# A two-layer MoE block on one Trainium2 core: how GpSimd gathers and scatters the expert rows

## The reference

```python
x = x + _L0_conv_ref(_ln_c(x), ...)            # attention and projection
t = _to_tokens(x)                              # 1536 rows of 256
t = t + _L0_ffn_ref(_ln_t(t), gate_w, gate_b, w1, b1, w2, b2)
...
# _L0_ffn_ref: top 2 of 8 experts, F = 1024
for i in range(e):
    h = jax.nn.silu(xf @ w1[i] + b1[i])
    out = out + (h @ w2[i] + b2[i]) * comb[:, i:i + 1]
# _L1_ffn_ref: top 2 of 8 experts, I = 672, gated
for e in range(E):
    a, g = jnp.split(x @ W1[e] + b1[e], 2, axis=-1)
    out = out + cw[:, e:e + 1] * (a * silu(g) @ W2[e] + b2[e])
```

## Time and profile before

| | |
|---|---|
| median of three runs | 581.94 us (581.19 to 582.55) |
| the profiled execution, its own time | 580.54 us |
| its span, first to last instruction | 578.8 us |
| PE busy | 535.1 us (92% of the span) |
| POOL busy | 275.2 us (48%) |
| DVE, ACT busy | 340.5 us (59%), 346.4 us (60%) |
| TensorE's mean granted clock, share of full | 0.974 |
| DMA, HBM read and written | 57.55 MB and 13.47 MB |

### The profile page before, as it was taken

The page is one execution under the profiler, slowest core; times in us unless marked ns, Lnnn a source line. Parts: engine busy times, 40 slices in busy tenths (PEclk is TensorE's granted clock), DMA queues, the critical chain, the costliest instruction groups (busy, mean ns, idle before and its releaser), DMA issues.

```text
span 578.8 us, 15638 instructions
## 1 busy us (share of the span) xinstructions
PE 535.1 (92%) x3521; PEld 471.4 (81%) x3522; DVE 340.5 (59%) x791; ACT 346.4 (60%) x676; POOL 275.2 (48%) x331
## 2 busy tenths in 40 slices
PE   8999968999999999999979996899999998999991
PEld 4887527999999889998868882599999998999881
DVE  5448864456533555554785488555777574667440
ACT  4777525666655666665468655456766765566430
POOL 4639131455655366664616340335465555444432
PEclk9999979999999999999989999799999999999996
DMA  8435867346432554236432157712547383222110
GB/s 274 147 118 160 265 190 247 105 118 155 113 74 35 142 118 89 34 82 175 141 121 95 57 153 264 258 33 43 136 129 190 80 226 86 36 75 46 27 24 10
DMA packets 49034, 70.50 MB, mean 122 GB/s; under 512 B 9182, under 2 KB 40560, under 8 KB 49008
## 3 DMA queue, kind: packets, MB, share of 16 engines
q1 hardware_dynamic: 35216, 56.41, 30.9%
q0 software_dynamic: 10464, 13.58, 13.8%
q10 hardware_dynamic: 3328, 0.20, 0.4%
HBM read 57.55 MB, written 13.47 MB: 123 GB/s over the span
## 4 chain that ended last, share of the span: by engine, by line
PE 63%; DMA 11%; DVE 9%; issue 6%; ACT 4%; POOL 2%; DVEq 1%; POOLq 1%; ACTq 0%; SPq 0%
PE banks L1302 14%; PE banks L1304 14%; PE banks L1303 14%; PE banks L1515 5%; PE banks L1343 5%; DMA out_dram<-expert_io,scol 5%; PE banks L1417 2%; DVE stats L909 2%; DMA expert_io<-xn_dram,gcol 2%; PE banks L1480 2%; DMA mid_dram<-expert_io,scol 1%; PE banks L1354 1%; ACT onehot_blk L805 1%; DVE xres L1060 1%; DMA xres<-in_x_dram 1%
## 5 line engine op out<-in xcount | busy, mean ns | idle before, releaser
L1302 PE MATMUL banks<-w_hi,xT_hi 128*128 x336 | 119.5, 356 | 4.1 <-DVE xT_lo L1175 2.6
L1304 PE MATMUL banks<-w_hi,xT_lo 128*128 x336 | 115.0, 342 | 0.0
L1303 PE MATMUL banks<-w_lo,xT_hi 128*128 x336 | 114.3, 340 | 0.0
L1302 PE MATMUL banks<-w_hi,hT_hi 128*128 x364 | 108.6, 298 | 3.1 <-DVE hT_lo L1250 3.0
L1304 PE MATMUL banks<-w_hi,hT_lo 128*128 x364 | 103.2, 284 | 0.0
L1303 PE MATMUL banks<-w_lo,hT_hi 128*128 x364 | 103.1, 283 | 0.0
L611 POOL TENSOR_TENSOR w_lo<-raw,w_hi 128x1024 fp32r<-128x1024 f32 (+2 forms) x24 | 58.9, 2468 | 50.8 <-ACT w_hi L688 43.2
L829 ACT COPY banks<-seed_rows 128x672 f32 (+1 forms) x84 | 69.0, 822 | 20.2 <-DVE h_sb L1267 9.1
L1302 PEld LDWEIGHTS banks<-w_hi,hT_hi 128*128 128x128 f32 x364 | 69.5, 191 | 6.8 <-issue 5.6
L627 POOL DMA_INDIRECT expert_io<-xn_dram,gcol x52 | 53.7, 1033 | 41.7 <-POOL gcol L623 37.7
L850 ACT CAST hT_hi<-banks 128x512 fp32r<-128x512 f32 (+1 forms) x112 | 55.4, 535 | 26.1 <-PE banks L1515 23.5
(11 more groups left out here) (208 smaller groups left out, 918.7 us busy)
## 6 DMA issues: line engine op xcount, KB each, us to landing
raw<-in_L_ffn_w_dram SPq DMA_DIRECT2D x32, 512.0 KB, 3.8
raw<-in_L_ffn_W_dram SPq DMA_DIRECT2D x16, 672.0 KB, 4.0
seed_rows<-in_L_ffn_b_dram SPq DMA_DIRECT2D x8, 672.0 KB
seed_rows<-in_L_ffn_b_dram SPq DMA_DIRECT2D x8, 512.0 KB
xn_dram<-raw SPq DMA_DIRECT2D x6, 512.0 KB, 3.0
raw<-in_L_ffn_W_dram SPq DMA_DIRECT2D x8, 384.0 KB, 3.4
raw<-in_L_ffn_W_dram SPq DMA_DIRECT2D x8, 256.0 KB
wqkv<-in_L_conv_W_qkv_dram SPq DMA_DIRECT2D x2, 768.0 KB, 6.6
```

Source lines behind the costliest of these rows:

```text
L1302: pe.matmul(out, hi, w_high, start=first, stop=False, skip_group_check=onto)
L1303: pe.matmul(out, hi, w_low, start=False, stop=False, skip_group_check=onto)
L1304: return pe.matmul(out, lo, w_high, start=False, stop=last, skip_group_check=onto)
```

## The change

- GpSimd no longer copies a row buffer: the scatter reads `y_rows` itself (`y_half`). `y_out` and `y_moved` are gone. VectorE now waits, before it writes a row buffer again, until the scatter that read it has landed (`added`).
- In `scatter`, the copy of the row numbers and the wait for VectorE's rows come before the wait for the scatter before; `scol` has four columns.
- Gathered rows have two buffers, the halves of `xg`, which blocks use in turn. `gather(b)` waits for the transposition of block `b - 2` instead of `b - 1`.
- Since which half is used is written into the instructions, the loops of GpSimd and TensorE do two blocks a turn. TensorE's conditional loop has two `If`s a turn and begins at step 22; GpSimd's conditional steps are written out, one after another.
- The last two blocks go to `last_y` in both layers; in layer 1 GpSimd scatters them from there.
- Four bias rows are in SBUF instead of three (`SEED_ROWS`). After that of expert 0, SP waits for both first gathers and then loads and awaits the other three, one after another; the weights of expert 4 come behind them. Later the bias row of expert `e - 1` goes with the weights of expert `e`, and only the last one is loaded by itself. `kT` moves into `region_d`.

```diff
@@ sync: after the rows are stored
                 load_seed(L, 0)
                 seed_loaded()
-                for e in range(1, SLOTS):
+                sp.wait_ge(s.gathered_first, 16)
+                sp.wait_ge(s.gathered, 16)
+                for e in range(1, SEED_ROWS):
                     load_seed(L, e)
-                for e in range(1, SLOTS):
                     seed_loaded()
                 expert_loaded(L, 0)
-                sp.wait_ge(s.gathered, 16)
                 load_expert(L, SLOTS + 1, 1)
...
-                            load_seed(L, e - 2)
+                            load_seed(L, e - 1)
...
-                for e in range(E - 2, E):
-                    sp.wait_ge(s.w_lo, PIECES * e + 1)
-                    load_seed(L, e)
-                    seed_loaded()
+                sp.wait_ge(s.w_lo, PIECES * (E - 2) + 1)
+                load_seed(L, E - 1)
+                seed_loaded()
@@ gpsimd
-                def gather(b):
+                def gather(b, half):
                     if after(b, 2):
-                        pool.wait_ge(s.xT_mm, b)
+                        pool.wait_ge(s.xT_mm, b - 1)
...
-                def scatter(b):
+                def scatter(b, rows, n):
+                    pool.tensor_copy(scol[:, n:n + 1], col(scatter_tab, b)).then_inc(s.scol, 1)
+                    pool.wait_ge(s.scol, b + 1)
+                    pool.wait_ge(s.e_sb, b + 1)
                     if after(b, 1):
                         pool.wait_ge(s.added, 16 * b)
-                    else:
-                        pool.wait_ge(s.tab, 3)
-                    pool.tensor_copy(scol[:, :], col(scatter_tab, b)).then_inc(s.scol, 1)
-                    pool.wait_ge(s.scol, b + 1)
-                    pool.wait_ge(s.e_sb, b + 1)
-                    pool.tensor_copy(y_out, y_sb(b)).then_inc(s.y_moved, 1)
-                    pool.wait_ge(s.y_moved, b + 1)
                     pool.sem_inc(rows_go, 1)
...
+                with pool.Fori(2, MIN_BLOCKS - 2, 2) as b:
+                    step(b)
+                    step(b + 1, 1)
+                for n in range(MIN_BLOCKS - 2, MAX_BLOCKS - 1):
+                    with pool.If(blocks > n + 1):
...
+                if L == 1:
+                    for n in range(2):
+                        scatter(blocks - 2 + n, last_y[n], 2 + n)
@@ vector
-                        if after(b, 3):
-                            dve.wait_ge(s.y_moved, b - 2)
-                        rows = xg if last else y_sb(b - 1)
-                        if L == 0 and (last or left == 1):
+                        if last or left == 1:
                             rows = last_y[int(last)]
+                        else:
+                            rows = y_sb(b - 1)
+                            if after(b, 3):
+                                dve.wait_ge(s.added, 16 * (b - 2))
@@ tensor
-                steps(pe, 2, 1, blocks, step)
+                with pe.Fori(2, MIN_BLOCKS - 2, 2) as b:
+                    step(b, 1)
+                    step(b + 1, 0)
+                with pe.Fori(MIN_BLOCKS - 2, MAX_BLOCKS, 2) as b:
+                    for n in range(2):
+                        with pe.If(b + n + 1 < blocks):
+                            step(b + n, 1 - n)
+                        with pe.Else():
+                            pe.nop()
```

83 lines of the change are left out of this document (39 added, 44 removed).

## The result

The changed kernel takes **572.06 us** (median of 4 runs, 571.91 to 572.61) against 582.25 us for the kernel before (4 runs beside it, 581.19 to 584.26): ratio 0.9847, 95% interval 0.9809 to 0.9885. The forecast was 575.2 us with a range of 572.0 to 580.3. The gain is 9.9 us counted from 581.94, the median that the forecast started from, and 6.7 had been forecast. The interval of the ratio is 6.7 to 11.1 us of gain, so the prediction's 0.2% for what a measurement can tell was too small.

The account below looks back on a forecast made before the run. TensorE, busy 92% of the span, was taken to set the time, with gains only where it waits for gathers and at the end. 5.0 + 0.8 + 0.6 - 0.2 + 0.5 = 6.7 us off 581.94 gave 575.2, range 572.0 to 580.3.

Parts of the forecast that it names:

- Layer 1 between blocks 2 and 27: Waits for gathers and the half clock behind block 18's stall go: 5.0 us gained, between 0 and about 6.
- Gather 18: Layer 1: issued some 2 us earlier, near 482.3, and landed by 485.2, before the bias row's load of 485.43 starts.
- Rival 1: Layer 1, block 18: the gather still meets the bias row's load, stall and clock remain; 2.4 us won, 579.5; chance 0.17.
- Layer 0 between blocks 3 and 27: Most of the 1.1 us lost in waits for gathers goes: 0.8 us gained; moved loads over first scatters cost 0.2.
- Start of layer 0: Waits of blocks 0 and 2 for their gathers, 0.37 and 0.29 us, both go: 0.6 us gained.
- Between the layers: Start of layer 1: no such idle time before its block 0 as in layer 0, so 0 gained.
- VectorE's new wait: Before writing block b, scatter b - 2 must have landed; 3.3 us to spare at the nearest row, so 0.
- rival 4: VectorE waits for scatters at each of about six bulk loads, 1 us each: 581.2, no change; chance 0.08.
- TensorE's loops: Fewer loop branches against more false `If`s after the last block: bounded by +0.6 to -0.6 us, taken as 0.
- Rival 3: TensorE's longer loop body waits for instruction fetch each turn of layer 1: 7.5 us, gain gone, 582.7; chance 0.04.
- The end: Row copy and hand-over leave the chain behind the last rows; last scatters start 0.5 us earlier, between 0.4 and 0.8.
- Rival 2: Start of each layer: moved loads hold scatter 0, making gather 4 late; 8.2 us lost, 583.4; chance 0.09.

Follow-up runs that it names:

- late gathers, old loads: Changed kernel with gathers waiting for the transposition of the block before and bias rows loaded in the earlier order: 574.6 us, ratio 0.9866.
- the bias rows alone: Kernel before with only the change's bias rows: four slots, rows of experts 1 to 3 loaded behind the first two gathers; 583.25 us, ratio 1.0045.
- the wait ahead of the numbers: Changed kernel, but GpSimd waits for the scatter before to land and only then copies row numbers, without the row copy: 576.73 us, ratio 0.9945.
- the copy beside the chain: Changed kernel with GpSimd's row copy put back into two buffers, ahead of the wait for the scatter before: 578.76 us, ratio 0.9940.
- late gathers: Changed kernel, but gather b waits for the transposition of block b-1 as before, moved bias rows kept: 579.71 us, ratio 0.9994.
- lead alone: Kernel before with only the second buffer of gathered rows and the two-block loops; old scatter chain and old loads: 584.24 us, ratio 1.0042.
- the paced kernel: Changed kernel with extra busy matmuls at each layer's start, and expert 4's weight parts loaded one per split piece: 575.1 us, ratio 0.9909.

## Why the prediction was right, point by point

The mechanism was right in the main: TensorE's waits for gathers, and the half clock behind the long one, are where the blocks of layer 1 gained. But the sum over the profile, 8.6 us where 6.7 had been forecast, has luck and canceled misses in it, as the terms show. Another 1.3 to 1.6 us lie between the profiles and the medians.

- **Layer 1 between blocks 2 and 27: 5.0 forecast, 5.13 measured.** Block 18's step gave 2.61, the one behind it 1.71, block 15 0.60 (forecast 2.6, 1.7, 0.5). Block 13 took 0.65 back, which had no term, and the other steps gave 0.86 where 0.2 was forecast, so the two misses cancel. The shorter chain of scatters is enough to remove the stall (late gathers, old loads), and the second buffer alone leaves it, as the prediction had it. What it did not have is that the moved rows alone remove it from block 18 as well, and pay with others at the start of both layers.
- **Gather 18, 2 us earlier forecast, 1.1 measured** against TensorE's blocks; that it goes at 480.17 and not at 482.3 comes from the earlier start of all of layer 1. It landed behind the start of the bias row's load, not ahead of it, in 2.8 us all the same, with 1.0 us to spare. Rival 1 did not come true, but it was nearer than the clean step of 6.58 us looks.
- **Layer 0 between blocks 3 and 27: 0.8 forecast, less 0.2 for the moved loads; 0.21 measured.** This term was mis-sized. The small waits of before went, but blocks 5 and 6 lost 0.7 us (7.29 and 6.85 instead of 6.71 each). The step that failed is the argument that a scatter among loads took 5.17 us: four parts of weights at once made it 7.17. It is not the moving of the rows that is to blame. With the old order of loads and the rest as changed this stretch takes 162.10 us: scatter 1, issued at 108.40, takes 8.4 us beside expert 5's loads (from 109.47 on), and blocks 5 and 6 take 7.06 and 6.86. The moved rows only chose which scatter meets a load. In layer 1 they may cost the 0.65 us of block 13, which doesn't wait with the old order.
- **Start of layer 0: 0.6 forecast, 1.6 measured.** The waits of 0.37 and 0.29 us are gone. I wrote that the busy matmuls bound the gain at block 0 to 0.4 us; block 0 is 0.89 us earlier, since besides the wait these matmuls took 3.85 us instead of 4.26: the clock was back at 83.97 instead of 84.74. Gather 2 is issued at 88.92, and no step of blocks 0 to 2 waits for a gather.
- **Between the layers: 0 forecast, 1.0 measured.** That is the half clock ahead of layer 1's blocks, above: 3.4 us in the changed kernel and 6.9 in the one before (361.2 to 368.1). Its length doesn't follow the change. It is the short one in the profile with the bias rows alone and in the one without them too, and the long one in those with the wait ahead of the numbers (359.8 to 366.7) and with the copy beside the chain (365.0 to 371.9), which have all the rest of the change. I count this 1.0 us, and 0.4 of layer 0's start, as what one profile happens to have: luck.
- **VectorE's new wait: 0, held.** In nine rows VectorE's idle time ahead of its row product ends with the landing of a scatter, which the prediction had named as a sign of being wrong. But it is 1.32 us at most there (at 127.11), and just as long at 140.54, where TensorE ends it, so the scatters held up next to nothing. TensorE's idle time behind VectorE's low parts of hidden rows is 3.9 us in seven places, before 3.0 in six; the new place is at 471.03, 0.38 us. None is behind the row product, so rival 4 is out. **TensorE's loops: 0, held:** undisturbed steps are 6.71 and 6.48 us as before, and the last conditional turns cost 7.90, 6.65 and 7.18 us (before 7.76, 7.10, 7.05). Rival 3 is out.
- **The end: 0.5 forecast, 0.65 measured.** The last scatters start at 556.96 and 561.50, from block 27's transposition on 0.5 and 0.6 us earlier than before.
- **Rival 2, the moved loads, was real and I had its condition nearly right.** It decides from a gather 3 us late, I wrote. With the lead two waits of 0.4 us are all; without it the stalls are 2.03 and 2.70 us, each with 3.4 us of half clock behind it, and the time is 579.7. So the chance of 0.09 was for a case that the second buffer kept away, whose worth the prediction had put low ("the gather gains only about 1.5 us"). The Trainium skill (DMA: Bandwidth & Descriptors, "Queues, rings and completion order") has the engines take turns between queues packet by packet; the trace agrees in kind, as the scatters among loads were slowed (7.17 and 10.05 us) and scatter 0 landed at 107.78, before SP, which awaits those loads, went on at 109.35. But "slowed" can be nearly threefold, and that stopped TensorE for 2.65 us.

## What to carry to other kernels

Where one engine's stream holds both the producer of the bound engine's data and a slower chain of its own, shorten what stands between one link of the chain and the next first: that gained clear of noise in three pairs of four here, and putting one small copy back behind the wait raised the median by 4.7 us, while a second buffer without it was worth nothing. Compare times within a step too, not by the clock alone, since everything behind an early gain is early. Judge the parts of a change together as well as apart, since a prefetch buffer can be worthless until the stream ahead of it is on time and then be what makes another part affordable. And before a load is moved, write down when each of the loads behind it is wanted: the bytes have to pass anyway, and each other order of them that was tried here put the wait elsewhere.

## What the runs showed of the hardware that was not expected

- A scatter of 128 rows (128 KB, accumulated in DRAM) takes 3.7 us at the end of layer 1, 7.17 among four weight loads of 512 KB each issued together, 7.98 at 434.14 us in the changed kernel, and 10.05 when the convolution's weights came first and expert 5's right behind.
- A standstill of TensorE doesn't always bring the half clock: behind 2.70 us (late gathers) and 2.77 us (lead alone) the next step took over 8 us, with a granted clock of 0.50 for 3.3 us of it at least (396.5 to 399.8, and 492.0 to 495.3), while behind the 2.65 us of the paced kernel it took 6.86, and the clock was 1.00:

```profile
137.00:146.00 9.00, 7.91 (x55) 1.00 0.87 251
```
- The half clock ahead of each layer's blocks lasted 3.4 or 6.9 us. Ahead of layer 0's, where the two kernels are alike up to there, it was 77.9 to 84.8 us in the kernel before and 78.9 to 82.4 in the one with the lead alone.
- Among the runs that the ratios use, the kernel before is spread over 574.9 to 584.0 us in the later experiments, several kernels between it and the changed one over 5 to 9 us, and the changed kernel's four runs over 0.7 us. That the spread goes with stalls that just happen or just don't is a guess: four runs are few, and the length of the half clock differs too.
